# Expert units of 128 rows instead of 256, loaded by a transposing DMA, with the feed-forward's two layers alternating by chunk

## What is computed

```python
# layer 0, condition: recurrence over 256 steps
gate = sigmoid(h @ Wh.T + z_t @ Wz.T + b);  h = tanh(h * (1 - alpha) + gate * z_t)
# layer 0, feed-forward: each of the 4096 rows goes through its 2 best of 8 experts
probs = softmax(hs @ gate_w + gate_b);  mask = one_hot(top_k(probs, 2)).sum(1) > 0
h1 = relu(hs @ w1[e] + b1[e]);  out = sum_e mask[:, e] * (h1 @ w2[e] + b2[e])      # 256 -> 1024 -> 256
x = x + out
# layer 1, condition: a shared expert (silu) and 8 routed ones (gelu), mixed by gates
# layer 1, feed-forward: activations in 256 levels, weights in int8 per channel
h = relu(quant_linear(x, w1, b1));  y = quant_linear(h, w2, b2)                    # 256 -> 1024 -> 256
x = x + y                                                                          # also around the condition's output
```

## Time and profile before

| | |
|---|---|
| three runs, median (lowest to highest) | 1268.68 us (1264.85 to 1269.13) |
| the profiled execution | 1267.8 us |
| its span, first to last instruction | 1264.8 us |
| mean granted TensorE clock | 0.987 |
| PE busy | 1123.6 us (89%) |
| PE weight loads | 864.7 us (68%) |
| DVE busy | 892.9 us (71%) |
| ACT busy | 583.3 us (46%) |
| POOL busy | 250.9 us (20%) |
| first layer of the experts, PE (L1105) | 1872 matmuls, 213.3 us busy |
| second layer of the experts, PE (L1117) | 1872 matmuls, 210.7 us busy |

### The profile page before, as it was taken

One profiled execution on the slowest core, in us unless ns is written; L12 is line 12 of the kernel. 1 busy time (PEld: TensorE's weight loads), 2 busy tenths in 40 slices (PEclk: granted clock), 3 DMA queues, 4 the chain that ended last, 5 costly groups with the idle time before them and its releaser, 6 DMA issues.

```text
span 1264.8 us, 32645 instructions
## 1 busy us (share of the span) xinstructions
PE 1123.6 (89%) x10732; PEld 864.7 (68%) x10733; DVE 892.9 (71%) x3002; ACT 583.3 (46%) x1782; POOL 250.9 (20%) x289
## 2 busy tenths in 40 slices
PE   6777777787768999999999999889999999987895
PEld 4665666565557999998899999746766666763263
DVE  5677677676775587965555555468898889987875
ACT  3555555555553444444444444362445533434373
POOL 1002112112114675343333333300000000001001
PEclk9999999999999999999999999989999999998998
DMA  6222333233233475343333333243000000000035
GB/s 174 76 72 89 90 97 97 82 93 109 71 91 106 102 166 133 91 70 59 58 53 60 62 62 62 36 132 134 2 1 1 0 1 0 1 1 1 1 51 83
DMA packets 57527, 84.36 MB, mean 67 GB/s; under 512 B 7361, under 2 KB 47170, under 8 KB 57410
## 3 DMA queue, kind: packets, MB, share of 16 engines
q1 hardware_dynamic: 41186, 57.94, 16.1%
q0 software_dynamic: 16224, 24.96, 10.9%
HBM read 51.36 MB, written 35.70 MB: 69 GB/s over the span
## 4 chain that ended last, share of the span: by engine, by line
PE 75%; ACT 9%; DVE 9%; issue 3%; DMA 1%; SPq 1%; POOL 0%; DVEq 0%; ACTq 0%; POOLq 0%
PE ps L570 23%; PE ps L1105 16%; PE ps L1117 16%; PE ps L1660 7%; DVE ps L1589 5%; PE ps L1665 4%; ACT work L1516 4%; ACT ps L1511 3%; DVE imax L986 2%; PE ps L924 2%; PE ps L1630 1%; PE ps L1086 1%; ACT W L955 1%; PE ps L1638 1%; PE ps L911 1%
## 5 line engine op out<-in xcount | busy, mean ns | idle before, releaser
L1141 ACT ACTIVATE lane<-ps,b_now 128x256 f32<-128x256 f32 x312 | 147.4, 474 | 240.1 <-PE ps L1105 216.4
L1105 PE MATMUL ps<-lane,W 128*128 128x256 f16 x1872 | 213.3, 274 | 2.2 <-ACT lane L1129 1.3
L1117 PE MATMUL ps<-W,lane 128*128 x1872 | 210.7, 273 | 0.0
L1105 PEld LDWEIGHTS ps<-lane,W 128*128 x1872 | 184.0, 98 | 25.1 <-issue 2.8
L1117 PEld LDWEIGHTS ps<-W,lane 128*128 128x128 f16 x1872 | 181.5, 98 | 20.4
L1660 PE MATMUL ps<-work 128*128 128x16 f16 x2048 | 99.1, 177 | 89.5 <-ACT work L1516 88.8
L1660 PEld LDWEIGHTS ps<-work 128*128 128x128 f16 x2048 | 76.3, 107 | 141.3 <-ACT work L1516 139.9
L1284 POOL DMA_INDIRECT results<-lane,dest x78 | 123.8, 1588 | 231.3 <-DVE lane L1198 195.8
L570 PE MATMUL ps<-W,work 128*128 128x512 f16 x768 | 168.7, 382 | 0.0
L1210 DVE TENSOR_TENSOR lane<-lane 128x256 f16<-128x256 f32 x312 | 133.4, 427 | 10.8
L570 PEld LDWEIGHTS ps<-W,work 128*128 128x128 f16 x768 | 74.9, 98 | 90.1 <-issue 2.2
(11 more groups left out here) (214 smaller groups left out, 1533.7 us busy)
## 6 DMA issues: line engine op xcount, KB each, us to landing
lane<-rows SPq DMA_DIRECT2D x39, 257.0 KB
stage<-in_w1T SPq DMA_DIRECT2D x16, 512.0 KB, 3.7
stage<-in_w2T SPq DMA_DIRECT2D x16, 512.0 KB, 4.0
b_now<-in_b SPq DMA_DIRECT2D x39, 128.0 KB
work<-in_zT SPq DMA_DIRECT2D x32, 128.0 KB, 2.2
results<-in_xn SPq DMA_DIRECT2D x32, 128.0 KB
W<-results SPq DMA_DIRECT2D x8, 512.0 KB, 3.8
out<-W SPq DMA_DIRECT2D x8, 512.0 KB, 4.9
```

The lines of the kernel that those rows point to most:

```text
L1105: last = pe.matmul(ps[:, f % 4, 0:ST], of_e(W1[:, bass.ds(e, 1), a, k, f * P:(f + 1) * P]), xT[:, p, b, k], start=(i == 0 and k == 0), sto ...
L1117: last = pe.matmul(ps[:, 4 + q, 0:D], hid[:, a, f, q * P:(q + 1) * P], of_e(W2[:, bass.ds(e, 1), b, f]), start=(i == 0 and f == 0), stop=( ...
L1141: act.activation(v4[:, f % 4], ps[:, f % 4, 0:ST], ACT.Relu, bias=b1_now[:, p, f:f + 1], scale=A_SCALE / W_SCALE).then_inc(l1_v, 1)
```

## The change

Units become ST = 128 rows: 71 units, rooms of 128 rows, 33 rooms an expert, 29 units written out, 20 passes of the loop, and two written out. The rows of a unit no longer come by rows to be transposed by PE: a transposing DMA, issued by SP, writes `xT` directly, and a small DMA brings the row numbers (`xg_tail`). PE's transposes and ACT's copies go. `v8` holds all eight chunks; DVE splits two chunks at a time. The second layer has three matmuls a chunk, and its results alternate between banks 4 and 5. DVE's jobs are spread over more units, one piece at a time. The core of it:

```diff
-ST = 256
+ST = 128
-JOBS = 15
-FIRST_JOB = 5
-EARLY = 16
+JOBS = 29
+FIRST_JOB = 10
+EARLY = 32
+PAIR = 2
...
         def experts_pe(pe):
-            def transposes(n, m, p):
...
             def tile(n, m, p):
                 if is_tile(n, JOBS - 1):
                     pe.wait_ge(table_ready, 2)
                 e = pe.value_load(expert_of[0:1, bass.ds(n, 1)], min_val=0, max_val=E - 1)
                 of_e = lambda a: a.rearrange("p a n -> p (a n)")
-                pe.wait_ge(xT_ready, n + 1)
+                pe.wait_ge(xT_in[p], 16 * m + 16)
                 for f in range(FC):
                     if not (is_tile(n, 0) and f < 4):
                         pe.wait_ge(l1_v, FC * n + f - 3)
...
                                              of_e(W1[:, bass.ds(e, 1), a, k, f * P:(f + 1) * P]), xT[:, p, b, k],
...
-                if not is_tile(n, SLOT_TILES - 1):
-                    transposes(n + 1, m + p, 1 - p)
-                if not is_tile(n, 0):
-                    pe.wait_ge(out_ready, n)
+                if not (is_tile(n, 0) or is_tile(n, 1)):
+                    pe.wait_ge(out_ready, n - 1)
                 for f in range(FC):
-                    pe.wait_ge(l1_hid, FC * n + f + 1)
+                    if f % PAIR == 0:
+                        pe.wait_ge(l1_hid, FC // PAIR * n + f // PAIR + 1)
                     for i, (a, b) in enumerate(((0, 0), (1, 0), (0, 1))):
                         for q in range(SQ):
-                            last = pe.matmul(ps[:, 4 + q, 0:D], hid[:, a, f, q * P:(q + 1) * P],
+                            last = pe.matmul(ps[:, 4 + SQ * p + q, 0:D], hid[:, a, f, q * P:(q + 1) * P],
                                              of_e(W2[:, bass.ds(e, 1), b, f]), start=(i == 0 and f == 0),
...
         def experts_act(act):
-                    if not (is_tile(n, 0) and f < 4):
-                        act.wait_ge(l1_hid, FC * n + f - 3)
-                    act.activation(v4[:, f % 4], ps[:, f % 4, 0:ST], ACT.Relu, bias=b1_now[:, p, f:f + 1],
+                    if f % PAIR == 0 and not is_tile(n, 0):
+                        act.wait_ge(l1_hid, FC // PAIR * (n - 1) + f // PAIR + 1)
+                    act.activation(v8[:, f], ps[:, f % 4, 0:ST], ACT.Relu, bias=b1_now[:, p, f:f + 1],
...
         def experts_dve(dve):
+                for h in range(FC // PAIR):
+                    pair = slice(PAIR * h, PAIR * h + PAIR)
+                    dve.wait_ge(l1_v, FC * n + PAIR * h + PAIR)
...
+                    dve.tensor_copy(hid[:, 0, pair], v8[:, pair]).then_inc(split0, 1)
+                    dve.wait_ge(split0, FC // PAIR * n + h + 1)
+                    dve.tensor_tensor(hid[:, 1, pair], v8[:, pair], hid[:, 0, pair], ALU.subtract).then_inc(l1_hid, 1)
+                    if isinstance(n, int) and n < len(LAST_OPS):
...
         def experts_pool(pool):
                     bias(n + 1, 1 - p, expert(n + 1))
+                if not is_tile(n, SLOT_TILES - 1):
+                    destination(n + 1, m + p, 1 - p)
                 if not is_tile(n, 0):
                     store_results(n - 1, 1 - p)
-                if not is_tile(n, SLOT_TILES - 1):
-                    destination(n + 1, m + p, 1 - p)
...
             def load_rows(r, p):
-                sp.dma_start(xg_rows[:, p], rows_d[bass.ds(r, 1)].rearrange("a (q p) n -> p (a q) n", p=P)).then_inc(xg_in[p], 16)
+                row = rows_d[bass.ds(r, 1)].rearrange("a r n -> (a r) n")
+                sp.dma_start(xg_tail[:, p], row[:, D - 1:D + 1]).then_inc(xg_in[p], 16)
+                sp.dma_start_transpose(xT[:, p].rearrange("p s k n -> p (s k) n"), row[:, 0:D].bitcast(F16))\
+                  .then_inc(xT_in[p], 16)
...
                     sp.wait_ge(dest_ready, n + 1)
-                    sp.wait_ge(xT_ps, n + 1)
+                    sp.wait_ge(l1_psum, FC * n + FC)
                     load_rows(ahead, p)
```

```diff
             def row_max(n):
-                pe.wait_ge(yq_T, 2 * n + 2)
+                pe.wait_ge(yq_T, 2 * n + 1)
...
                     last.then_inc(ia_ps, 1)
+                    if f in (2, 5) and 2 * n + 2 + f // 5 < GROUPS:
+                        transposes(2 * n + 2 + f // 5)
...
             def group(g, buf):
+                    for f in range(FC):
+                        hidden(g + 1, f)
+                        wait_rounded(pe, g, f)
+                        for q in range(GT):
+                            last = output(buf, f, q)
```

The last two groups (g >= ADDED = 6) are finished in SBUF, where x plus bias is added by DVE (`x_with_bias`, `outputs`), and stored by SP in halves of 256 KB:

```diff
+            for n in range(2 * ADDED, 2 * GROUPS):
+                sp.wait_ge(ob, n + 1)
+                sp.dma_start(out[:, 2 * n:2 * n + 2], y[:, 2 * n:2 * n + 2]).then_inc(last_out, 16)
```

More of the change, by code:

```diff
@@ L295, in build_program @@
         xg_in = [sem(f"xg_in{i}") for i in range(2)]
-        xT_ps = sem("xT_ps")
-        xT_ready = sem("xT_ready")
+        xT_in = [sem(f"xT_in{i}") for i in range(2)]
         out_ready = sem("out_ready")
@@ L881, in row_max @@
                     for m in range(2):
+                        if f == 0 and m == 1:
+                            pe.wait_ge(yq_T, 2 * n + 2)
                         for k in range(DC):
@@ L894, in ffn_pe @@
             largest(0)
-            for n, groups in enumerate((range(0, 3), range(3, 6), range(6, 8), ())):
-                for g in groups:
-                    transposes(g)
+            for g in range(2):
+                transposes(g)
+            for n in range(GROUPS // 2):
                 row_max(n)
@@ L904, in ffn_pe, with hidden @@
             pe.wait_ge(ia_mx, FC * GROUPS // 2)
[L906 to L913, removed]
+            def hidden(g, f):
+                if not (is_tile(g, 0) and f < 4):
+                    pe.wait_ge(hb_h, FC * g + f - 3)
+                for k in range(DC):
+                    last = pe.matmul(ps[:, f % 4], w1qT[:, k, f * P:(f + 1) * P], yqT[:, k, bass.ds(GN * g, GN)],
+                                     start=(k == 0), stop=(k == DC - 1))
+                last.then_inc(hb_ps, 1)
@@ L915, in group, with output @@
+            def output(buf, f, q):
+                return pe.matmul(ps[:, 4 + 2 * buf + q // 2, (q % 2) * D:(q % 2 + 1) * D],
+                                 hq[buf][:, f, q * P:(q + 1) * P], w2qT[:, f], start=(f == 0 and q % 2 == 0),
+                                 stop=(f == FC - 1), skip_group_check=True)
             def group(g, buf):
-                if not is_last(g):
-                    hidden(g + 1)
                 if not is_tile(g, 0) and not is_tile(g, 1):
                     pe.wait_ge(ob_s, 2 * (g - 1))
-                for q in range(GT):
-                    for f in range(FC):
[L922 to L927, removed]
@@ L929, in ffn_pe @@
-            hidden(0)
+                if is_last(g):
+                    for half in range(2):
+                        for f in range(FC):
+                            if half == 0:
+                                wait_rounded(pe, g, f)
+                            for q in (2 * half, 2 * half + 1):
+                                last = output(buf, f, q)
+                        last.then_inc(ob_ps, 1)
+                else:
+                    for f in range(FC):
+                        hidden(g + 1, f)
+                        wait_rounded(pe, g, f)
+                        for q in range(GT):
+                            last = output(buf, f, q)
+                            if f == FC - 1 and q % 2:
+                                last.then_inc(ob_ps, 1)
@@ L930, in ffn_pe @@
+            for f in range(FC):
+                hidden(0, f)
             ffn_groups(pe, group)
@@ L938, in ffn_act, with quantised @@
             act.wait_ge(inv_ready, 1)
-            for g in range(GROUPS):
+            def quantised(g):
                 act.activation(y8[:, g], y[:, GT * g:GT * g + GT].rearrange("p q d -> p (q d)"), ACT.Relu,
                                scale=inv[:, 0:1]).then_inc(yq_m, 1)
-                if g >= 2:
-                    transposed(g - 2)
-            transposed(GROUPS - 2)
+            for g in range(GROUPS):
+                quantised(g)
+                if g == 1:
+                    transposed(0)
+                if g == 1 or g >= 3:
+                    transposed(g if g == 1 else g - 1)
             transposed(GROUPS - 1)
@@ L1029, in group @@
                     hidden(g + 1, 1 - buf, None if is_tile(g, 0) else (g - 1, 1 - buf))
+                    if is_tile(g, 0):
+                        dve.wait_ge(bq_ready, 3)
+                        for k in range(ADDED, GROUPS):
+                            x_with_bias(k)
             hidden(0, 0)
-            dve.wait_ge(x_out, 16 * GROUPS)
+            dve.wait_ge(x_out, 16 * ADDED)
             dve.wait_ge(wt_cp, 5)
@@ L1438, in tile @@
                     at = n - FIRST_JOB
-                    for c in range(2 * at + 2, min(2 * at + 4, 8)) if at < 4 else range(at + 4, min(at + 5, len(pieces))):
-                        load_piece(c)
+                    if at < 7:
```

(3 more changed lines are left out.)

201 lines of the change are left out of this document (101 added, 100 removed).

## The result

The kernel after takes 1385.4 us (median of 4 runs, 1383.0 to 1385.9), the kernel before, on the same chip, 1267.7 (4 runs, 1264.9 to 1269.1): a ratio of 1.093, 95% interval 1.090 to 1.095, so 118 us slower. The forecast was 1379, between 1318 and 1438.

A forecast was written before the change was run, and what follows sets the result against it. PE's sequencer was taken to bound the changed expert stage: 545 + 3 + 3 - 1.5 - 429.6 = +120 us; with -9.3 elsewhere, 1267.8 + 120 - 9.3 = 1378.5, plus 0.9 for the median: 1379 us, range 1318 to 1438.

The forecast's parts named there:

- The bound: Expert stage: PE's sequencer limits 128-row units, with 48 regops (FUSED_REGOPS, register instructions) a unit at 0.125 us each; 80%.
- Written-out units: Expert stage, 31 units outside the loop: 1.0 + 47 x 0.125 + 0.1 = 7.0 us each.
- Loop units: Expert stage, 40 units in the loop: 8.2 us each, including nine ALU_OPs at 0.8 us.
- First unit: Start of the expert stage: 3 us extra left for slow matmuls, and a start 1.5 us earlier.
- The 3 us for routing operations: Expert stage, units 0 to 4: two routing operations after each DVE pair add 3 us in all.
- near 925: Sign of being right: the expert stage would end near 925 us.
- Hidden things: Expert stage: ACT, DVE, POOL's accumulating stores and the transposing DMA run behind PE's sequencer and add nothing beyond routing.
- The wait for the last pair of hidden rows: Between a unit's layers: rows ready about 1.5 us after first-layer issue, needed 12 regops (1.5 us) in; nothing taken.
- the rival of the lower level: Expert stage: TensorE falls to 1.2 GHz, 10.6 us a unit, about 1587 us in all; 3%.
- Edges: Parts outside the expert stage (start, last maximum, row maxima, feed-forward, end): together -9.3 us.
- row maxima: After the mixture: 4.3 of DVE's 6.3 us of waits for PE removed, leaving about 2 us.
- feed-forward: Feed-forward layers alternating by chunk: net -2.7 us, between -5 and +1, groups 7.0 us apart.

The follow-up runs named there:

- the two runs with the number loaded early: Next unit's expert number loaded between the layers: kernel after, 1378.9 us; kernel after with constant first-layer addresses, 1234.4 us.
- the run without register work: Kernel after, with PE taking expert 0's weights for every unit, so addresses are constant and no expert number is loaded: 1221.5 us, ratio to before 0.964.
- the run with 40 regops: Kernel after, same result, second layer with one 512-column matmul for the high part, 40 FUSED_REGOPS a unit instead of 48: 1343.2 us.
- the edges alone: Kernel before with only the changes outside the expert stage (start, last maximum, row maxima, feed-forward, final stores): 1256.2 us, ratio 0.992.
- the profile with expert 0: Kernel before, with PE taking expert 0's weights for every unit: 1266.5 us, ratio 0.999.

## Why the prediction was right, and where it was off

**The bound.** Right: the regops are 71 x 48, 0.124 apart, and the time falls with their number (48, 40, none: 1385, 1343, 1222) while the array's work stays.

**Written-out units.** 7.20 us instead of 7.0. The starts are 0.124 apart, but five times a unit there are 0.03 to 0.07 more and once 0.15, which I had not counted. 30 x 0.2 = +6 us.

**Loop units.** 8.28 instead of 8.2, with ten ALU_OPs instead of nine: +3.4.

**First unit.** 13.2 instead of 10.0 (7.0 + 3): +3.2. The timeline (start, length, engine, line, idle before) shows ACT stop for 3.9 us with finished chunks in PSUM, and PE behind it:

```profile
383.58 0.37 ACT L1164 ACTIVATE lane<-ps,b_now 128x128 f32<-128x128 f32 x1 [0.66 <-PE ps L1135]
...
387.84 0.37 ACT L1164 ACTIVATE lane<-ps,b_now 128x128 f32<-128x128 f32 x1 [3.90 <-issue]
388.34 0.57 PEld L1135 LDWEIGHTS ps<-lane,W 128*128 x6 [2.90 <-issue]
```

In the two runs with the number loaded early this stop isn't there. In the kernel before it is: ACT's operations on the first unit start at 386.78 and then 390.80, and its first unit takes 14.6 us instead of 10.93, so the 3 us that the prediction left for slow matmuls weren't theirs alone. What ACT waits for in the stop stays open. The 3 us for routing operations didn't come: the units 1 to 4 are 6.9 to 7.5. Altogether (+6, +3.4, +3.2, -3) the stage took 560.7 us instead of 551 and ended at 942.4 instead of the sum's 933.5 (the "near 925" among the signs was a slip against my own sum).

**Hidden things.** DVE, ACT, POOL's stores and the transposing DMA were hidden. The DMA still is at 5.3 us a unit, as the run without register work shows: there SP begins to issue it 7.2 us (median; at least 6.3) before the first layer that reads the rows, and PE doesn't wait for it. DVE is not hidden everywhere in that run. The wait for the last pair of hidden rows, at which the prediction took nothing, cost nothing: the regop behind it starts 0.12 us after its predecessor (median of the written-out units); with six regops in front of it instead of twelve it costs 0.2 to 0.6 us, as the run with 40 regops shows. TensorE's clock stayed at 1.00, 2.4 GHz, in the loop, so the rival of the lower level falls.

**Edges.** Predicted -9.3. From segment to segment of the two profiles: row maxima 51.1 to 47.2 us, -3.9 (predicted -4.3); feed-forward 64.7 to 63.2, -1.5 (predicted -2.7), its groups 7.15 apart instead of 7.5:

```profile
1340.06 0.60 PE ps L923 x2
...
1347.21 0.60 PE ps L923 x2
```

DVE's wait at the row maxima is 2.3 us, as forecast near 2, and the last store landed 3.2 us after its issue (forecast 3.4), the shortest of the four:

```profile
DVE imax L1014 <- PE ps L894: 2.3, 1, 2.3
```

```profile
DMA to landing us min/median/max: 3.2/4.1/5.1
```

The end came to -3.7, 2.7 of it in the landing and 1.0 in what follows it. Not foreseen: -2.3 between the stage and the mixture, because a unit of 128 rooms ends with one accumulating store instead of two; +0.7 in the mixture. At the start I had taken 0; with the edges alone the stage begins 1.9 us earlier (382.1 instead of 384.0), which is most of why that kernel gained 11.2 rather than 8.4. After minus before is so +128.8 - 2.3 + 0.7 - 3.9 - 1.5 - 3.7 = 118.1, the difference of the spans (1382.9 - 1264.8). The stage came out 9 us longer than the sum and the edges gave 1.4 us more than foreseen, from terms that partly cancel: the 6 us between forecast and result are that close in part by luck.

**The range.** The working calls 618 us the most for the units, but the range was built on 603; with 618 its upper end would have been 1452. The result lies inside either.

## What to carry to other kernels

```profile
PEclk7555555555558999999999999989999999998998
...
L1630 PE MATMUL ps<-work 128*128 128x128 f32 x256 | 98.0, 488 | 7.3 <-DVE gw_s L1565 7.3
```

```profile
PEclk9999999999999999999999999989999999998998
...
L1630 PE MATMUL ps<-work 128*128 128x128 f32 x256 | 98.3, 490 | 7.5 <-DVE gw_s L1565 7.5
```

So PE ran alike in both, and no run shows what the other level would make of the recurrence. The length of a matmul tells the level where the row has nothing. In the profile with expert 0 the row goes from half to full at 387.0, and there the 256-column matmuls of L1105 go from 421 to 272 ns. In the kernel before they go from 418 to 273 ns at about 388.7, with a row of 1.00 on both sides, so its first unit begins at the lower level, 1.2 GHz; in the kernel after the same change (421 to 273 ns) comes at 393.3.

- SP's instruction for a transposing DMA holds its queue much longer than a plain one (0.34 us for the stores above), by source line:

```profile
L1428 SPq DMA_TRANSPOSE lane<-rows x71: 922/1218/2159, 364.6 to 925.2; - x71
```

Left open: a version that jumps to one of eight copies of PE's code by the expert's number, so that units of 128 rooms have constant addresses and the right expert (the 1221.5 us above are without the choice), wasn't run, and neither was any other way to get there.
